# Cross-attention of a decoder layer: values product in three float32r passes, probabilities scaled on GpSimd

## What is computed

```
x = x + self_attention(layernorm(x))              # 4 x 1024 rows of 256, 16 heads
x = x + cross_attention(layernorm(x), ctx, ctx, mask)
x = x + mixture_of_experts(x)                     # row norm, gate, top 2 of 8, shared expert
# cross_attention: 16 heads of 64, 77 keys per batch
scores  = (q @ k^T) / 8 ; scores = where(mask == 0, -1e10, scores)
weights = softmax(scores) ; out = (weights @ v) @ Wo
```

## Time and profile before

| what | us |
|---|---|
| median of three runs | 1705.21 |
| the profiled execution | 1713.24 |
| its span | 1711.5 |
| last unit of VO out of PSUM, end of `phase_context` | about 857 |
| cross-attention, transposes of tile 0 to transposes of tile 31 | 875.84 to 1170.36 |
| last of the cross pipeline, experts start | about 1186 |

### The profile page before, as it was taken

How to read it: one execution, slowest core, us unless ns; L and a number is a source line. 1 busy time by engine, 2 the same in 40 slices (tenths; PEclk the granted TensorE clock), 3 DMA queues, 4 the chain that set the end, 5 groups by cost and what they waited for, 6 DMA issues and landing times. The chain is left out here.

```text
span 1711.5 us, 35350 instructions
## 1 busy us (share of the span) xinstructions
PE 1663.2 (97%) x11830; PEld 1092.0 (64%) x11831; DVE 1381.4 (81%) x2605; ACT 1097.7 (64%) x2272; POOL 395.4 (23%) x464
## 2 busy tenths in 40 slices
PE   7899999999999999999989999997999999999998
PEld 3443333333333333358678999996898888888887
DVE  6788999999999999926678889994887666666664
ACT  5336888888888888872567777874335545454552
POOL 2000000000000000023042222222562555554540
PEclk9858999999999999999999999998999999999999
DMA  6601112221111111012311222113725333333335
GB/s 218 197 11 21 31 31 39 38 36 33 33 31 31 31 30 30 3 43 75 119 44 45 101 67 84 49 50 118 244 76 167 53 55 50 55 49 55 50 58 169
DMA packets 85147, 116.41 MB, mean 68 GB/s; under 512 B 19051, under 2 KB 64415, under 8 KB 84415
## 3 DMA queue, kind: packets, MB, share of 16 engines
q1 hardware_dynamic: 67248, 90.95, 19.2%
q0 software_dynamic: 13728, 18.88, 6.7%
q10 hardware_dynamic: 4047, 4.91, 0.9%
HBM read 71.25 MB, written 46.60 MB: 69 GB/s over the span
## 5 line engine op out<-in xcount | busy, mean ns | idle before, releaser
L506 DVE TENSOR_REDUCE half_max<-psA 128x1 f32<-128x512 f32 x1024 | 630.9, 684 | 20.1 <-PE psA L559 18.1
L538 ACT ACTIVATE PT<-psB 128x1024 f32<-128x1024 f32 x512 | 520.8, 1026 | 154.0 <-PE psB L569 153.5
L559 PE MATMUL psA<-KS,QS 48*128 48x512 f32 x1024 | 404.9, 479 | 8.2 <-PEq L104 2.5
L569 PE MATMUL psB<-QS,KS 50*128 50x512 f32 x1024 | 384.8, 465 | 0.1
L588 PE MATMUL psO<-PT,VG 128*32 128x256 f32 x4096 | 327.6, 399 | 0.1
L559 PEld LDWEIGHTS psA<-KS,QS 48*128 48x128 f32 x1024 | 166.6, 195 | 238.9 <-DVE half_max L506 178.0
L588 PEld LDWEIGHTS psO<-PT,VG 128*32 128x32 f32 x4096 | 85.2, 109 | 180.4 <-issue 109.3
L1390 ACT ACTIVATE x_probs<-x_scores,x_neg_max 128x77 f32<-128x77 f32 x512 | 176.3, 358 | 6.8 <-DVE x_neg_max L1293 6.6
L569 PEld LDWEIGHTS psB<-QS,KS 50*128 50x128 f32 x1024 | 154.0, 189 | 10.7 <-ACT PT L538 9.5
L1872 PE MATMUL m_psY<-swd_high,m_hT 128*128 128x256 f32 x760 | 157.6, 290 | 0.3 <-DVE m_hT L2026 0.2
L475 POOL CAST max_parts<-neg_max 128x16 fp32r<-128x16 f32 x32 | 6.3, 196 | 632.1 <-DVE neg_max L516 632.1
(11 more groups left out here) (235 smaller groups left out, 2702.5 us busy)
## 6 DMA issues: line engine op xcount, KB each, us to landing
QS<-q_parts SPq DMA_DIRECT2D x96, 128.0 KB
q_parts<-part SPq DMA_DIRECT2D x16, 512.0 KB, 4.4
mx_kept<-cx_mx SPq DMA_DIRECT2D x8, 616.0 KB, 4.9
cx_mx<-mx_kept SPq DMA_DIRECT2D x4, 1232.0 KB, 7.4
KS<-k_parts SPq DMA_DIRECT2D x32, 128.0 KB
xf_rows<-XF SPq DMA_DIRECT2D x32, 128.0 KB, 1.7
acc<-X SPq DMA_DIRECT2D x32, 128.0 KB, 1.8
xf_turned<-n_xfT SPq DMA_DIRECT2D x32, 128.0 KB, 1.8
```

Source lines behind the costliest of these rows:

```text
L506: dve.tensor_reduce(half_max[:, h * (TB // 2) + t % (TB // 2), n:n + 1], psA[:, bank_of(slot, 2 * v + r), :], axis=AX.X, op=ALU.max).then_ ...
L538: act.activation(PT[:, k % 4, 2 * a:2 * a + 2, :].rearrange("p h n -> p (h n)"), psB[:, u % 2, :, :].rearrange("p a n -> p (a n)"), ACT.Ex ...
L559: pe.matmul(psA[:, bank_of(slot, m), :], QS[top:top + KQ, slot, h // 2, t * P:(t + 1) * P], KS[top:top + KQ, slot, n * HALF:(n + 1) * HALF ...
L569: mm = pe.matmul(psB[:, u % 2, r, :], KS[top:top + KM, slot, c * P:(c + 1) * P], QS[top:top + KM, slot, a, half * HALF:(half + 1) * HALF], ...
```

## The change

- VO is float32r in two parts, high and low, and has two slots instead of four batches. Batches 0 and 1 are split by ACT and DVE when they are made; batches 2 and 3 are left raw in a new table VR, and GpSimd splits them later, at stage L_Y of tiles 8 to 14 and 16 to 22, when the slot's old batch is done.
- The transposed probabilities get a high part (ACT, as before) and a low part (DVE, three subtracts from psE). The product with the values becomes 30 float32r matmuls: high x high, high x low, low x high.
- DVE no longer scales the probabilities. GpSimd does, in two halves of eight heads, after a reciprocal of each half by DVE.
- The row maximum moves from L_SM to L_S of the step before, and comes out negative at once; the factor 1/8 goes into the keys.
- In DVE's list the reciprocals and the maximum stand behind the low part of the turned row and ahead of XF. In GpSimd's list the second half's scaling stands behind the fill, the first half's scaling between the two L1160 norms.
- XF has two slots instead of 32 tiles and waits for its store of two tiles before; WU's high part gets a place of its own. GpSimd's list is written out step by step instead of as a loop.

```diff
 # phase_context, ACT and DVE taking VO out of PSUM
+            for n in range(1, RAW, 2):                      # RAW = 10 of 20 units, batches 2 and 3
+                dve.wait_ge(r_done, n + 1)
+                dve.tensor_copy(raw(n), back(n)).then_inc(r_in[1], 1)
+            for n in range(RAW, len(BACKS)):
+                dve.wait_ge(r_in[0], n - RAW // 2 + 1)
+                dve.tensor_tensor(part_of(n, 1), back(n), part_of(n, 0), ALU.subtract).then_inc(r_in[1], 1)
...
 # phase_cross, GpSimd
+            def scale_probs(t, half):
+                i, e = t
+                first, last = HEADS[half]
+                pool.wait_ge(recip_done, 2 * i + half + 1)
+                probs = by_head(PX, e)[:, first:last, :]
+                pool.tensor_tensor(probs, probs, over_keys(recip[:, e, first:last]), ALU.mult).then_inc(scaled, 1)
+            def split_values(slot, c):
+                n = slot * NPK + c
+                pool.tensor_copy(VO[:, slot, 0, c, :], VR[:, slot, c, :]).then_inc(vo_split, 1)
+                pool.wait_ge(vo_split, 2 * n + 1)
+                pool.tensor_tensor(VO[:, slot, 1, c, :], VR[:, slot, c, :], VO[:, slot, 0, c, :], ALU.subtract).then_inc(vo_split, 1)
...
-                    pool.memset(SX[:, e, :], NEG_RAW).then_inc(filled, 1)
+                    pool.memset(SX[:, e, :], NEG).then_inc(filled, 1)
...
+                if t := tile(L_E):
+                    scale_probs(t, 1)
                 if (t := tile(L_LN)) and not peeled(t[0], NORMED):
...
-                for n, lag in enumerate((L_Y, L_XF)):
+                def own_rstd(n, lag):
...
+                own_rstd(0, L_Y)
+                if t := tile(L_Y):
+                    slot, j = t[0] // TB - 1, t[0] % TB
+                    if slot in (0, 1) and j < SPLIT_STEPS:
...
+                        for c in range(j * NPK // SPLIT_STEPS, (j + 1) * NPK // SPLIT_STEPS):
+                            split_values(slot, c)
+                if t := tile(L_SM):
+                    scale_probs(t, 0)
+                own_rstd(1, L_XF)
...
 # PE
-                    pe.wait_ge(scaled, at(i, 1, 1))
+                    pe.wait_ge(scaled, at(i, 2, 2))
...
-                        mm = pe.matmul(psY[:, 0, 0:D], ET[:, c, :], VO[:, i // TB, c, :], start=(c == 0), stop=(c == NPK - 1))
+                    for a, b in PRODUCTS:
+                        for c in range(NPK):
+                            if c % 4 == 0 and (a, b) != PRODUCTS[1]:
+                                pe.wait_ge(e_low if a else e_in, at(i, 3, c // 4 + 1))
+                            mm = pe.matmul(psY[:, 0, 0:D], ET[a][:, c, :], VO[:, slot, b, c, :],
...
 # DVE
+            def head_sums(t, half):
+                i, e = t
+                first, last = HEADS[half]
+                dve.wait_ge(exp_done, at(i, XH, last))
+                dve.reciprocal(recip[:, e, first:last], row_sum[:, e, first:last]).then_inc(recip_done, 1)
...
-                dve.tensor_reduce(row_max[:, e, :], by_head(SX, e), axis=AX.X, op=ALU.max).then_inc(max_done, 1)
-                dve.tensor_scalar(neg_max[:, e, :], row_max[:, e, :], -XSCALE, None, ALU.mult).then_inc(neg_done, 1)
-                dve.reciprocal(recip[:, :], row_sum[:, e, :]).then_inc(recip_done, 1)
-                dve.tensor_tensor(by_head(PX, e), by_head(PX, e), over_keys(recip[:, :]), ALU.mult).then_inc(scaled, 1)
...   # behind the masked copies (L_S):
+                if t := tile(L_E):
+                    i, e = t
+                    for n, (first, tiles) in enumerate(EBANKS):
+                        dve.wait_ge(e_in, at(i, 3, n + 1))
+                        dve.tensor_tensor(ET[1][:, first:first + tiles, :], psE[:, n, 0:tiles * P]..., ET[0][...], ALU.subtract).then_inc(e_low, 1)
...   # behind the low part of the turned row (L_XT):
+                if t := tile(L_SM):
+                    head_sums(t, 0)
+                if t := tile(L_S):
+                    i, e = t
+                    dve.wait_ge(s_in, at(i, 3, 3))
+                    dve.tensor_reduce(neg_max[:, e, :], by_head(SX, e), axis=AX.X, op=ALU.max, negate=True).then_inc(neg_done, 1)
+                if t := tile(L_SM):
+                    head_sums(t, 1)
                 if t := tile(L_XF):
                     dve.wait_ge(n_rstd_done[0], at(i, 1, 1))
+                        dve.wait_ge(kept[e], at(i - e, 16, 0))
+                    dve.tensor_scalar(XF[:, e, :], X[:, i, :], n_mean_var[:, 0, e, 0:1], n_rstd[:, e:e + 1],
```

More of the change, by code:

```diff
@@ L821, in phase_context @@
         UNITS = NPR * KD
-        BACK = B * NPK // 2
+        BACKS = [(b, pair) for b in (2, 3, 0, 1) for pair in range(NPK // 2)]
+        RAW = 2 * (NPK // 2)
         BACK_RING = 4
@@ L910, in _ @@
             pe.wait_ge(padded, 1)
[L911 to L914, removed]
+            for n, (b, pair) in enumerate(BACKS):
+                m = n - BACK_RING
+                if m >= RAW:
+                    pe.wait_ge(r_in[1], m - RAW // 2 + 1)
+                elif m >= 0:
+                    pe.wait_ge(r_in[m % 2], m // 2 + 1)
                 for half in range(2):
@@ L921, in back, with raw, part_of @@
         def back(n):
-            b, pair = divmod(n, NPK // 2)
-            return VO[:, b, 2 * pair:2 * pair + 2, :], bank_back(n).rearrange("p (c n) -> p c n", n=D)
+            return bank_back(n).rearrange("p (c n) -> p c n", n=D)
+        def raw(n):
+            b, pair = BACKS[n]
+            return VR[:, b - 2, 2 * pair:2 * pair + 2, :]
+        def part_of(n, part):
+            b, pair = BACKS[n]
+            return VO[:, b, part, 2 * pair:2 * pair + 2, :]
         @block.vector
@@ L978, in _ @@
                 act.activation(pair_columns(VT[:, :, u % KD, :], u // KD), pair_banks(u + UNITS), ACT.Copy).then_inc(p_in[0], 1)
+            for n in range(0, RAW, 2):
+                act.wait_ge(r_done, n + 1)
+                act.activation(raw(n), back(n), ACT.Copy).then_inc(r_in[0], 1)
             act.wait_ge(mx_in, MX_KEPT)
-            for n in range(0, BACK, 2):
+            for n in range(RAW, len(BACKS)):
                 act.wait_ge(r_done, n + 1)
-                to, source = back(n)
-                act.activation(to, source, ACT.Copy).then_inc(r_in[0], 1)
+                act.activation(part_of(n, 0), back(n), ACT.Copy).then_inc(r_in[0], 1)
 def phase_cross(nc, T):
-    X, XF, LG, ident, MX, VO = T["X"], T["XF"], T["LG"], T["ident"], T["MX"], T["VO"]
+    X, XF, LG, ident, MX, VO, VR = T["X"], T["XF"], T["LG"], T["ident"], T["MX"], T["VO"], T["VR"]
     mx_kept, mx_in = T["mx_kept"], T["mx_in"]
@@ L1005, in phase_cross @@
         PX = sb("x_probs", [P, 2, NPK * P])
-        row_max = sb("x_row_max", [P, 2, XH])
         neg_max = sb("x_neg_max", [P, 2, XH])
         row_sum = sb("x_row_sum", [P, 2, XH])
-        recip = sb("x_recip", [P, XH])
-        ET = sb("x_ET", [P, NPK, P])
+        recip = sb("x_recip", [P, 2, XH])
+        ET = [sb(f"x_ET{part}", [P, NPK, P], F32R) for part in range(2)]
         gate = sb("gate_sb", [P, KD, NE])
@@ L1161, in step @@
                         pool.wait_ge(n_rstd_done[n], at(i, 1, 1))
-            staggered(pool, NT, LAGS, step)
+                own_rstd(0, L_Y)
+                if t := tile(L_Y):
+                    slot, j = t[0] // TB - 1, t[0] % TB
+                    if slot in (0, 1) and j < SPLIT_STEPS:
+                        if j == 0:
+                            pool.wait_ge(y_done, TB * (slot + 1))
+                        for c in range(j * NPK // SPLIT_STEPS, (j + 1) * NPK // SPLIT_STEPS):
[3 more added lines that the diff above has]
+                own_rstd(1, L_XF)
+            for n in range(NT + max(LAGS)):
+                step(lambda lag, n=n: (n - lag, (n - lag) % 2) if 0 <= n - lag < NT else None)
         @block.tensor
@@ L1322, in step @@
                     dve.sem_inc(T["waited_dve"], 1)
-                    take_stats(0, own, X)
+                    take_stats(0, own, X[:, i, :])
                 for stage in (aggregate, add_eps):
@@ L1499, in expert_places @@
     T["split"] = []
-    for weight, tokens in (("WG", "X"), ("WU", "XF")):
+    for weight, tokens in (("WG", "X"), ("WU", "WU_high")):
         high, low = (nc.alloc_sbuf_tensor_at(f"m_{place}_split", [P, NE, KD, FI], F32R, offset=T["place"][place])
```

72 lines of the change are left out of this document (34 added, 38 removed).

## The result

The changed kernel takes 1743.16 us (median of 4 executions, 1737.89 to 1744.68), the kernel before 1703.81 us (4 executions, 1699.01 to 1707.19). The ratio is 1.022, its interval 1.018 to 1.026: slower by 39.4 us, where the prediction had 48.5, and inside its range of 1725 to 1788. The profiled execution of the changed kernel took 1744.68 us, with a span of 1743.0 and a mean granted clock of 0.971.

A forecast was written before the change was run, and what follows sets the result against it. PE's own order bounded the kernel before; after the change, a circle of waits through all engines would. Terms 44.2 + 1.1 + 4.0 - 0.8 = +48.5 us on the median of 1705.2 gave 1754 us, range 1725 to 1788.

The forecast's parts named there:

- The circle: Cross-attention: waits through ACT's exponentials, DVE's reciprocal and XF, GpSimd's norm, fill and scaling, PE's transposes; 11.16 us per step.
- The scaling of 616 elements: GpSimd's scaling of half the probabilities, a shape no profile row had: taken as 1.40 us, between 1.23 and 2.05.
- the other four: Cross-attention steps outside the 27 from tile 2 to 29: first 9.5 us, second 8.5, last two about 9.7 each.
- Rival (c): Cross-attention: PE's pauses drop its clock to the low level, +190 us more; chance 0.01.
- DVE's sum: DVE's work per cross-attention step stays at 9.3 us, so PE's own 8.85 is not reached.
- rival (a): Cross-attention: the circle of waits opens somewhere, engine sums hold; 1699 us, or 1683 if DVE is quicker; chance 0.10.
- The context loop: Making the values in `phase_context`: ten units need ACT then DVE, 12.95 us instead of 8.93, +4.0; bounds +2.9 and +9.5.
- Ahead of the first E and behind the last: E is PE's transposes of the probabilities: +1.1 us before tile 0's for the fill, -0.8 after the last for the product.
- The shared port: GpSimd can hold DVE off at SBUF; the new subtracts and masked copies were said not to be held.
- (b): Cross-attention: DVE's masked copies and GpSimd's second scaling exclude each other; 11.84 us per step, +19 more, 1773; chance 0.08.
- (d): Little change: DVE bound at 9.6 to 9.7 us per step, waits partly hidden, 1705 to 1730 us; chance 0.07.

The follow-up runs named there:

- pe_busy: The changed kernel with the score matmuls of bank 3 issued twice, so PE pauses less: 1745.99 us, ratio 1.0259 to the kernel before.
- both_orders: The changed kernel with GpSimd's L_XF norm one step later and DVE's XF part ahead of both reciprocals and the maximum: 1680.75 us, ratio 0.9888.
- norm_later: The changed kernel with GpSimd's row norm of stage L_XF one step later, behind the scaling and the other norm: 1709.17 us, ratio 1.0023.
- odd_widths: norm_later with DVE's XF and xn each computed in two pieces of 127 and 129 columns: 1714.2 us, ratio 1.0075.
- two_inputs: norm_later with XF computed by a DVE operation reading two tensors from SBUF instead of one: 1681.04 us, ratio 0.9893.

## Why the prediction was right

**The circle: shown.** Each of its links showed up in the profile after, and the two reorderings that cut it give back 34 and 42 us, together 62. Lengthening it by a fill costs 35.8.

**Its size: 10.78, not 11.16.** The scaling of 616 elements was the unknown price. I took 1.40 us between 1.23 and 2.05; it is 1.22, the lower bound, 0.18 less. XF to the norm took 1.68 instead of 1.84. The rest is gaps: 0.12 instead of 0.28 from the reciprocal to XF. Against these, E to the reciprocal took 0.07 more (5.77, against 5.70) and the norm to the fill 0.08 more (0.73, against 0.65). Over 27 steps -0.38 each is -10.3 us. But the 27 steps are 10.92 in the mean, not 10.78, which is +3.8. Of the other four, the first was 10.11 instead of 9.5 (+0.6) and the last two 9.1 instead of 9.7 (-1.2). From the predicted +44.2 this leads to the measured +37.2, but for rounding. So the total came out closer than the 10.3 us of the mis-sized links alone would have had it, by terms that I hadn't foreseen; that part is luck.

**The longer steps: not foreseen, and mostly not the clock.** From tile 8 to tile 26 every second step is 10.91 to 10.97 us (11.28 at tile 8): in them XF starts 0.31 us behind the second reciprocal, not 0.12. Two steps have one more delay: at tile 4 the norm starts 2.06 us behind XF instead of 1.68 (step 11.14), at tile 8 the fill 1.05 behind the norm instead of 0.73. pe_busy has all of these at the same tiles, with its clock at 1.00. The clock made two steps longer, 12.09 at tile 15 and 11.17 at tile 23, where pe_busy has 10.78 and 10.77: 1.7 us together. Rival (c) had the clock fall for good. It neither did that nor stayed up. PE paused for 1.97 us ahead of E at 1008.71; then the windows show 0.50 at 1010 to 1012 and 1.00 again from 1014, and the product in between took 5.09 us instead of 3.67. PE had slack of some 2 us per step, which took most of it. The prediction's row for a pause without a fall, 868 to 876 of the earlier trace rows, was no guide to this place. Nor does the length of the pause alone decide: behind pauses of 1.98 us ahead of E at 986.98 and 1.97 ahead of E at 1075.21 the clock stayed at 1.00.

**DVE's sum: wrong, without harm.** I said 9.3 us per step and that 8.85 is not reached. In both_orders DVE is busy 180.84 us in 200 / 8.77 = 22.8 steps, 7.9 a step, and 8.77 is reached. Of these 1.4 us, 0.6 lie in the start: in the kernel before DVE was busy 179.81 of 200 us (940 to 1140), 8.70 a step, and my 9.3 took the step less the one idle time that the timeline showed, so it counted DVE's short waits as work. The largest other part lies in work that was long only beside the fill. Before, the negative maximum took 0.95 us a step and the reciprocal 0.83, their records overlapping; the two reciprocals of both_orders take 0.40. My sum had only 0.32 for this exchange. The sum entered only rival (a), whose place of decision was right: the fill free to start behind the last exponential. Its price was not: with both edits the kernel runs at 1680, near its second figure of 1683 and not its first of 1699.

**The context loop: +2.2, not +4.0.** The pace of DVE's ten units was the term. The timeline of the loop after, beside the earlier trace rows:

```profile
839.61 0.60 ACT L991 ACTIVATE VR<-psPc 128x512 f32<-128x512 f32 x1 [1.40 <-PE psPc L919]
...
848.26 1.27 DVE L972 TENSOR_TENSOR VO<-psPc,VO 128x512 fp32r<-128x512 f32 x2
849.46 1.27 DVE L972 TENSOR_TENSOR VO<-psMc,VO 128x512 fp32r<-128x512 f32 x2
```

From the first row to the end of the last it is 850.73 - 839.61 = 11.1 us, against 8.93. Pairs of subtracts start 1.20 us apart, 0.60 a unit, where I had taken 0.80 and, as the lower bound, 0.69: the duration of one, though the records of neighbours overlap. So +2.2 lies below the bound of +2.9. A pace is read from start to start.

**Ahead of the first E and behind the last: +1.3 and -0.4**, for +1.1 and -0.8.

**The shared port.** The changed kernel does not pay for it in the circle: no link runs beside a GpSimd instruction that holds it. (Ahead of the circle's steps three xn took 1.27 us instead of 0.40.) As soon as the circle was cut on one side only (norm_later), it did: about 1.2 us per step, XF 1.27 - 0.41 and xn 0.78 - 0.40, and DVE's list became the bound. The Trainium skill, page "SBUF — State Buffer", section "Who interferes with whom", has tensor_scalar among the operations that take the shared pair, and says that a DVE instruction with two inputs in SBUF is not held by a GpSimd instruction that only writes. The traces agree with both: 1273 ns for the one form beside the fill, 480 for the other. The Trainium skill's page "VectorE: DVE Perf Modes", section "Mode 2×_2P — use both read ports for one tensor", admits odd widths when source and destination are equal. I had read past that in odd_widths, and the times of its two pieces, 1.42 and 1.21 us, agree with the page.

**The other rivals.** (b), masked copies and scaling excluding each other: no; all 64 scalings of the changed kernel, those beside the copies among them, took 1214 to 1222 ns. (d): no, by the interval.

**Still open.** Why XF starts 0.19 us later in every second step from tile 8 on; why only some of PE's pauses of 2 us are followed by the lower clock; and why norm_later has steps of about 10.22 and 9.84 in turn from tile 10 on. two_inputs, which frees XF alone, brings these to 8.76 and 8.89, so XF being held is needed for most of their length.

## What to carry to other kernels

When work moves to an engine with plenty of idle time, don't ask whether it fits; follow one turn from the bound engine through every in-order list back to it, and count what is queued ahead of the instruction that closes the turn. A short instruction that waits late (here a norm of 0.55 us) belongs behind the work that is ready earlier, even a whole step later. If all engines show idle time in one window, the cure is an order, and the sums by engine then say what it can bring: here 1680 us instead of 1743, from the same instructions.

## What the runs showed of the hardware

- A DVE tensor_scalar of 128x256 float32 from SBUF to SBUF takes 0.41 us alone and 1.27 beside GpSimd's memset; it ends some 0.15 us after the memset does. With widths of 127 and 129 it is held as well. scalar_tensor_tensor with two SBUF inputs takes 0.48 beside the same memset.
- A DVE reciprocal of 128x8 that starts during the same memset takes 0.19 us (14 cases in both_orders), and 0.19 during GpSimd's subtract of 128x256 (5 cases in the changed kernel): it is not held. The reciprocals of the kernel before, 0.63 us in the median, probably only stood in line behind the negative maximum, which was.
- GpSimd's in-place multiply of 128x616 float32 with a broadcast factor takes 1.22 us, DVE's 0.80.
- After PE's pause of 1.97 us ahead of 1008.71 a stretch at a granted clock of 0.50 (the level of 1.2 GHz) followed, and 1.00 (2.4 GHz) again by 1014; after other pauses of 1.97 and 1.98 us it stayed at 1.00. With pe_busy's pauses of 0.83 to 1.36 us (E's of tiles 3 to 29) it stayed at 1.00 up to 1196.
